# Graph kernel: the keys of the edges are asked for five batches ahead, into six buffers, instead of two batches ahead into three

## The chip, the cores and the metric

The program runs on one core of a Trainium2 chip. The metric is device time in microseconds (us), from one launch of the whole program. Engines are called as the profile calls them: PE (TensorE), DVE (VectorE), ACT (ScalarE), POOL (GpSimd), SP (SyncE).

## The reference

The input is a graph of 1250 nodes with 768 features and 20000 edges, sorted by target node. A GCN layer (layer 0) is followed by a relational graph attention module of two layers, with 4 heads (layer 1) and 1 head (layer 2), and three relations. Both parts are residual.

```python
def rgat_conv(x, W, q, k, b, src, dst, etype, heads, out_ch, n_nodes):
    xr = jnp.einsum('nd,rdf->rnf', x, W)
    oi = xr[etype, dst]
    oj = xr[etype, src]
    qi = oi @ q
    kj = oj @ k
    alpha = jax.nn.leaky_relu(qi + kj, NEG_SLOPE)
    m = jax.ops.segment_max(alpha, dst, num_segments=n_nodes)
    e = jnp.exp(alpha - m[dst])
    z = jax.ops.segment_sum(e, dst, num_segments=n_nodes)
    a = e / (z[dst] + EPS)
    msg = (a[:, :, None] * oj.reshape(-1, heads, out_ch)).reshape(-1, heads * out_ch)
    out = jax.ops.segment_sum(msg, dst, num_segments=n_nodes)
    return out + b
...
h = jnp.maximum(_layernorm(x, axis=-1), 0.0)
x = x + _L0_gnn_ref(h, edge_index, L0_gnn_W, L0_gnn_b)
h = jnp.maximum(_layernorm(x, axis=-1), 0.0)
x = x + _L1_gnn_ref(h, edge_index, edge_type_3, ...)
```

## The kernel before, in words

The 1250 nodes are 10 tiles of 128. The sorted edges lie in slots, 128 to a column. Two columns are a pair, and a pair holds edges of one target tile only. These inputs fill 83 pairs. The target tiles are very uneven: the first has 26 pairs (0 to 25), the second 11 (26 to 36), the third 8 (37 to 44), and the last seven have 7, 6, 6, 5, 5, 5 and 4.

Each attention layer l (1 and 2) has these parts. All of them but the last run in one stretch, which the rest of this text calls the score stretch of the layer.

- POOL fetches, for each column of 128 edges, the key `kj` of each edge's source from a table in DRAM, by one indirect DMA per column (`ask_keys`, line L519). Twelve columns (6 pairs) are a batch. When a batch is there, `score` adds the query and applies the leaky ReLU in three short POOL instructions (L529, L533, L537), which release the batch's six pairs to DVE through the semaphore `al_step`. The number of gathers in flight is bounded by separate semaphores, `k_in`, of which there are `KFLIGHT`: 4 in layer 1, 2 in layer 2. Gather t waits until gather t - 4 (or t - 2) has landed. Thirteen batches (0 to 12, `KSURE`) are written out one after the other, the last one (13) is in a loop whose count depends on the data, and ran once here. The batches lie in `kb`, which has `KSEMS` slots.
- DVE gets the queries of the edges ready (`qs_ready`, behind L977) and then builds, pair by pair, the running maximum of each target tile: a subtraction or addition (L1017 in layer 1, L1023 in layer 2), and a maximum (L1020, L1028). After the last pair of a tile it raises `z_in`, and `maxima` finishes the tile before (L990 to L996).
- PE multiplies the nodes by the three relations' weights, 30 steps of one node tile each (`project`, L1320). After some of the steps it also turns a tile's running maximum around (L1338) and spreads finished maxima back to the edges (L1236, L1233). These places are fixed, in the order of PE's program, by the table `MAX_AT`: tile 0 after step 11, tile 1 after step 14, tile 2 after step 17, then after steps 19, 21, 23, 25, 27, 28, and the last after step 29. PE waits there for `z_in`, and for the reading of the tile before.
- The last part gathers whole rows of 768 features (L488, POOL), scales them (DVE) and sums them with one-hot matmuls (PE, L1359 or L1361 and L1362). POOL can't begin before PE has passed all of the maxima and DVE has formed the exponents' arguments (the semaphore of L1348).

POOL's order in the score stretch is: wait for the keys' table, ask for two batches, wait for `qs_ready`, then score batch n and ask for batch n + 2, until 13 batches are asked for and scored. The places in the code are these.

```python
MAX_AT = {11: (0,), 14: (1,), 17: (2,), 19: (3,), 21: (4,), 23: (5,), 25: (6,), 27: (7,), 28: (8,), 29: (9, 10, 11)}
...
KSEMS = 3
KFLIGHT = {1: 4, 2: 2}
```

Of the kernel before, what the change touches and what calls it, by code (L numbers as in the profile page):

```python
# [40 lines left out]
NPAIR = R * NT * PAIRS_STEP  # L41
KB = 4 * PAIRS_STEP
KBATCHES = 2 * NPAIR // KB
KSEMS = 3
KFLIGHT = {1: 4, 2: 2}
assert all(KB % n == 0 for n in KFLIGHT.values())
assert KBATCHES * KB == 2 * NPAIR
KSURE = ((E + PAIR - 1) // PAIR - 1) // (KB // 2)
# [54 lines left out]
def gnn_kernel(nc, x, src, dst, edge_type, W0, b0, W1, q1, k1, b1, W2, q2, k2, b2, out):  # L103
# [12 lines left out]
    with ExitStack() as ctx:  # L116
# [124 lines left out]
        qe = ringf[:, 0:T * R * 4]  # L241
        kb = ringf[:, T * R * 4:T * R * 4 + KSEMS * KB * 16].rearrange("p (a t c) -> p a t c", a=KSEMS, c=16)

# [99 lines left out]
        def load_bounds(eng):  # L343

            eng.wait_ge(bounds_ready, 1)
            return [0] + [eng.value_load(bounds[0:1, j:j + 1], min_val=j if j < NT else (E + PAIR - 1) // PAIR, max_val=MAXPAIRS) for j in range(1, NT + 1)]
# [107 lines left out]
        @block.gpsimd  # L454
        def _(pool):
            nc.gpsimd.iota(iota_f[:, :], [[1, T]], base=0, channel_multiplier=0, allow_small_or_imprecise_dtypes=True).then_inc(pool_c, 1)
            nc.gpsimd.iota(iota_h[:, :], [[1, T]], base=0, channel_multiplier=0, allow_small_or_imprecise_dtypes=True).then_inc(pool_c, 1)
            nc.gpsimd.iota(iota_p[:, :], [[0, 1]], base=0, channel_multiplier=1, allow_small_or_imprecise_dtypes=True).then_inc(pool_c, 1)
            nc.gpsimd.memset(half[:, :], -0.5).then_inc(pool_c, 1)
            nc.gpsimd.memset(zero16[:, :], 0.0).then_inc(pool_c, 1)  # L460
            nc.gpsimd.memset(ones[:, :], 1.0).then_inc(pool_c, 1)
            nc.gpsimd.memset(idxr[:, T:T + KB], 0).then_inc(pool_c, 1)
            pool.wait_ge(pool_c, 7)
            bnd = load_bounds(pool)
            pool.wait_ge(slots_f, 1)
            pool.sem_inc(turn, 1)

            def targets(first, end):
                for c in range(first * PB, end * PB):

                    pool.wait_ge(perm_free, c + PB + 1)
                    pool.sem_inc(turn, 1)
                    nc.gpsimd.tensor_scalar(oh_tg[:, c % PB, :], iota_h[0:EP, 0:P], dloc[:, c:c + 1], None, ALU.is_equal).then_inc(tg_in, 1)  # L473

            targets(0, 1)
            pool.wait_ge(var_ready, 1)
            nc.gpsimd.tensor_tensor(rstd[:, :], vare[:, :], half[:, :], ALU.pow).then_inc(rstd_ready, 1)
            targets(1, GROUPS)
            pool.wait_ge(deg_ready, 1)
            nc.gpsimd.tensor_tensor(dinv[:, :], deg[:, :], half[:, :], ALU.pow).then_inc(dinv_ready, 1)  # L480
            groups = (bnd[NT] + (RING - 1)) // RING
            rest = (bnd[NT] + (RING - 1 - RING * FIXED)) // RING

            def gather_rows(l, idx):

                for t in range(2 * RING * FIXED):
                    pool.wait_ge(w_used[l], t + 1)
                    nc.gpsimd.indirect_dma_start(ring[:, t % (2 * RING), 0:WIDTH[l]], None, rows[l], bass.IndirectOffsetOnAxis(idx[:, t:t + 1], 0)).then_inc(g_sem[l][t % (2 * RING)], 16)  # L488

                with pool.Fori(0, rest) as g:  # L490
                    for side in range(2):

                        pool.wait_ge(g_in[l], 2 * RING * g + (2 * RING * FIXED + RING * side + 1))
                        nc.gpsimd.tensor_copy(idxs[:, RING * side:RING * (side + 1)], idx[:, ds(g * (2 * RING) + (2 * RING * FIXED + RING * side), RING)]).then_inc(ix[l], 1)
                        pool.wait_ge(ix[l], 2 * g + (side + 1))
                        pool.sem_inc(turn, 1)
                        for s in range(RING * side, RING * (side + 1)):
                            if s % 2 == 0:

                                pool.wait_ge(w_used[l], g * (2 * RING) + (2 * RING * FIXED + s + 2))  # L500
                                pool.sem_inc(turn, 1)
                            nc.gpsimd.indirect_dma_start(ring[:, s, 0:WIDTH[l]], None, rows[l], bass.IndirectOffsetOnAxis(idxs[:, s:s + 1], 0)).then_inc(g_sem[l][s], 16)

            pool.wait_ge(slots_ready, 1)
            pool.wait_ge(s_rows0, 16 * (NT + 1))
            gather_rows(0, idx0)
            pool.wait_ge(var_ready, 2)
            nc.gpsimd.tensor_tensor(rstd[:, :], vare[:, :], half[:, :], ALU.pow).then_inc(rstd_ready, 1)
            for l in (1, 2):
                H = HEADS[l]  # L510

                flight = KFLIGHT[l]

                def ask_keys(n):

                    for t in range(n * KB, (n + 1) * KB):
                        if t >= flight:
                            pool.wait_ge(k_in[l][t % flight], 16 * (t // flight))
                        nc.gpsimd.indirect_dma_start(kb[:, n % KSEMS, t % KB, 0:4], None, keys[l], bass.IndirectOffsetOnAxis(idxr[:, t:t + 1], 0)).then_inc(k_in[l][t % flight], 16)  # L519

                def score(n, slot, lows, looped=False):

                    batch = al[:, ds(n * (KB * H), KB * H)]
                    for s in range(flight):
                        pool.wait_ge(k_in[l][s], n * (16 * KB // flight) + 16 * KB // flight)
                    if looped or n > 0:
                        pool.wait_ge(al_step[l], n * (KB // 2))
                    pool.sem_inc(turn, 1)
                    nc.gpsimd.tensor_tensor(summed[:, 0:KB * H].rearrange("p (c h) -> p c h", h=H), kb[:, slot, :, 0:H], qs[:, ds(n * (KB * H), KB * H)].rearrange("p (c h) -> p c h", h=H), ALU.add).then_inc(k_sum[l], 1)  # L529
                    pool.wait_ge(k_sum[l], n + 1)  # L530
                    if looped:
                        pool.sem_inc(turn, 1)
                    nc.gpsimd.tensor_scalar(low[:, 0:KB * H], summed[:, 0:KB * H], 0.0, SLOPE - 1.0, ALU.min, ALU.mult).then_inc(k_low[l], 1)  # L533
                    pool.wait_ge(k_low[l], lows)
                    if looped:
                        pool.sem_inc(turn, 1)
                    nc.gpsimd.tensor_tensor(batch, summed[:, 0:KB * H], low[:, 0:KB * H], ALU.add).then_inc(al_step[l], KB // 2)  # L537

                pool.wait_ge(g_in[l - 1], 2 * RING * groups + (RING + 1))
                pool.sem_inc(turn, 1)  # L540
                pool.wait_ge(s_keys, 16 * R * l)
                ask_keys(0)
                ask_keys(1)
                pool.wait_ge(qs_ready, l)
                for n in range(KSURE):
                    score(n, n % KSEMS, n + 1)
                    if n + 2 < KSURE:
                        ask_keys(n + 2)


                with pool.Fori(1, (bnd[NT] + (255 - (KSURE + 1) * (KB // 2))) // 256 + 2) as m:
                    n = m + (KSURE - 1)
                    nc.gpsimd.tensor_copy(idxk[:, :], idxr[:, ds(n * KB, KB)]).then_inc(k_low[l], 1)
                    pool.wait_ge(k_low[l], m * 2 + (KSURE - 1))
                    pool.sem_inc(turn, 1)
                    for k in range(KB):
                        pool.wait_ge(k_in[l][k % flight], n * (16 * KB // flight) + 16 * (k // flight))
                        pool.sem_inc(turn, 1)
                        nc.gpsimd.indirect_dma_start(kb[:, KSURE % KSEMS, k, 0:4], None, keys[l], bass.IndirectOffsetOnAxis(idxk[:, k:k + 1], 0)).then_inc(k_in[l][k % flight], 16)
                    score(n, KSURE % KSEMS, m * 2 + KSURE, True)  # L560
                for side in range(2):
                    pool.wait_ge(stage_out[l][side], 16 * R * NT // 2)
                pool.wait_ge(rows_go[l], 1)
                gather_rows(l, idxr)
# [826 lines left out]
```

## Time and profile before

| | us |
|---|---|
| median of the runs | 1615.69 |
| the runs | 1609.24, 6044.12, 1615.69 |
| the profiled execution | 1607.11 |
| its span, first to last instruction | 1605.3 |
| mean granted TensorE clock in it | 0.932 of full |

The rows below come from the profiled execution. Its span is 1.8 us shorter than its time; the median of the runs is 8.6 us above it. One of the three runs lies far off the others and has no part in what follows. Of the span, the score stretch of layer 1 is from 469 us (the first gather of keys) to 780 us (the first gather of rows), that of layer 2 from 1063 us to 1365 us.

A row of a timeline gives the start in us, the duration in us, the engine, the line, the operation, what it writes and reads, how many equal instructions the row stands for, and in brackets how long the engine had been idle and what ended that.

### The profile page before, as it was taken

The page shows a single profiled execution, that of the slowest core. Times are in us where ns is not written, and L with a number is a line of the kernel's source. Part 1 is how long each engine was busy: PE and PEld are TensorE (multiplying, and loading weights), DVE is VectorE, ACT ScalarE, POOL GpSimd, SP SyncE. Part 2 cuts the span into 40 slices and gives each one's busy share as a digit, 9 for nine tenths or more (in the row PEclk, how much of TensorE's full clock was granted, in tenths as well). Part 3 has the DMA queues.
Part 4 walks back from the last instruction along what each step waited for, and adds up shares of the span by engine and source line. Part 5 has one row for each costly group of instructions (what it writes and reads, how often), then busy time and mean ns, then how long its engine had stood idle before and what let it go on. Part 6 is the DMA issues. An engine that isn't in the chain of part 4 may idle for free.

```text
span 1605.3 us, 24837 instructions
## 1 busy us (share of the span) xinstructions
PE 1453.7 (91%) x6446; PEld 878.0 (55%) x6450; DVE 901.0 (56%) x2002; ACT 274.0 (17%) x709; POOL 1000.9 (62%) x1112
## 2 busy tenths in 40 slices
PE   4988999999978999999699999769996999899996
PEld 2545555555566555666455555455553655455553
DVE  8677722334455888888688878406324445223333
ACT  2545300000011333323000124410110011000000
POOL 1599277666537777882477777336656662777673
PEclk9988999999987999899799999858997999899998
DMA  8300498899831131111588888701231111889898
GB/s 319 118 20 21 125 315 305 291 316 312 270 102 23 51 110 47 40 37 41 169 303 278 285 262 257 241 3 32 59 111 31 40 43 50 286 298 308 281 303 269
DMA packets 86811, 271.80 MB, mean 169 GB/s; under 512 B 32156, under 2 KB 32531, under 8 KB 86743
## 3 DMA queue, kind: packets, MB, share of 16 engines
q0 software_dynamic: 51072, 199.44, 39.3%
q1 hardware_dynamic: 34807, 65.62, 11.4%
q10 hardware_dynamic: 864, 5.90, 1.0%
q8 instruction: 35, 0.57, 0.2%
q14 instruction: 33, 0.27, 0.1%
HBM read 239.28 MB, written 31.62 MB: 169 GB/s over the span
## 4 chain that ended last, share of the span: by engine, by line
PE 61%; DMA 14%; POOL 10%; issue 7%; DVE 5%; ACT 1%; DVEq 1%; SPq 0%; POOLq 0%; ACTq 0%; PEldq 0%
PE ps L1293 12%; PE ps L1320 12%; PE ps L1359 12%; DMA ring<-keys,idxr 8%; POOL ring L519 8%; PE ps L1361 6%; PE ps L1362 6%; PE ps L1190 5%; DMA ring<-rows,idxr 3%; PE ps L1111 1%; PE ps L1236 1%; PE ps L1153 1%; PE ps L1254 1%; DVE zw L1020 1%; DVE hn L1017 1%
## 5 line engine op out<-in xcount | busy, mean ns | idle before, releaser
L1320 PE MATMUL ps<-wreg,hT 128*128 128x384 f32 x1440 | 486.7, 501 | 7.3 <-PEq L1313 6.6
L519 POOL DMA_INDIRECT ring<-keys,idxr x312 | 319.2, 1023 | 189.1 <-DMA ring<-keys,idxr 73.6
L488 POOL DMA_INDIRECT ring<-rows,idxr x304 | 303.7, 999 | 168.8 <-PEq L1348 60.9
L1320 PEld LDWEIGHTS ps<-wreg,hT 128*128 128x128 f32 x1440 | 280.6, 196 | 202.2 <-issue 23.5
L1359 PE MATMUL ps<-ring,zw 128*128 x664 | 224.0, 495 | 15.6 <-DVE zw L1088 15.0
L1293 PE MATMUL ps<-ring,zw 128*128 x664 | 221.3, 495 | 9.6 <-DVE zw L909 9.6
L488 POOL DMA_INDIRECT ring<-rows,idx x152 | 144.7, 952 | 97.1 <-PE ps L1293 66.0
L1359 PEld LDWEIGHTS ps<-ring,zw 128*128 128x128 f32 x664 | 124.7, 191 | 108.7 <-issue 34.2
L1086 DVE TENSOR_TENSOR ring<-ring,al x166 | 159.2, 959 | 39.4 <-SPq L406 30.7
L1293 PEld LDWEIGHTS ps<-ring,zw 128*128 128x128 f32 x664 | 127.5, 193 | 98.1 <-issue 15.3
L1091 DVE TENSOR_SCALAR zw<-iota_f,tl,al 128x128 f32<-128x128 f32 x166 | 60.8, 368 | 154.7 <-PE ps L1362 129.7
L909 DVE TENSOR_SCALAR zw<-iota_f,tl,ring 128x128 f32<-128x128 f32 x166 | 58.6, 358 | 154.8 <-PE ps L1293 140.0
L1361 PE MATMUL ps<-ring,zw 128*128 x332 | 136.3, 492 | 9.9 <-DVE zw L1091 9.7
L473 POOL TENSOR_SCALAR stT<-iota_h,stT 125x128 f16<-125x128 f16 x160 | 106.4, 683 | 49.7 <-DVEq L799 28.1
L1362 PE MATMUL ps<-ring,zw 128*128 x332 | 135.2, 489 | 0.0
L1017 DVE TENSOR_TENSOR hn<-al,hn 128x1024 f32 x83 | 101.7, 1225 | 35.4 <-POOL al L537 15.5
L1023 DVE TENSOR_TENSOR hn<-hn,al 128x256 f32 x83 | 35.6, 429 | 143.8 <-POOL al L537 127.8
L1020 DVE TENSOR_TENSOR zw<-zw,hn 128x1024 f32<-128x1024 f32 x83 | 101.8, 1227 | 2.9
L1361 PEld LDWEIGHTS ps<-ring,zw 128*128 128x128 f32 x332 | 62.5, 191 | 53.4 <-issue 13.5
L1362 PEld LDWEIGHTS ps<-ring,zw 128*128 128x128 f32 x332 | 63.4, 191 | 44.3 <-issue 0.6
L1190 PE MATMUL ps<-ring,hT 128*128 128x384 f32 x240 | 86.0, 513 | 0.0
L659 ACT ACTIVATE hn<-iota_f,tlb 128x128 f32<-128x128 f32 (+1 forms) x166 | 56.8, 393 | 119.2 <-DVE hn L1017 105.7
(189 smaller groups left out, 1314.0 us busy)
## 6 DMA issues: line engine op xcount, KB each, us to landing
wreg<-in_L_gnn_W SPq DMA_DIRECT2D x11, 2304.0 KB, 9.8
rows<-stage SPq DMA_DIRECT2D x30, 386.0 KB, 2.8
rows<-stage SPq DMA_DIRECT2D x30, 384.5 KB, 2.9
stT<-targets_row ACTq DMA_DIRECT2D x6, 960.0 KB
ring<-keys,idxr POOLq DMA_INDIRECT x312, 2.5
ring<-rows,idxr POOLq DMA_INDIRECT x304, 4.5
rows<-stT SPq DMA_DIRECT2D x10, 384.0 KB, 2.9
xs<-in_x SPq DMA_DIRECT2D x3, 1152.0 KB, 13.4
```

The source lines that it names most:

```text
L473: nc.gpsimd.tensor_scalar(oh_tg[:, c % PB, :], iota_h[0:EP, 0:P], dloc[:, c:c + 1], None, ALU.is_equal).then_inc(tg_in, 1)
L488: nc.gpsimd.indirect_dma_start(ring[:, t % (2 * RING), 0:WIDTH[l]], None, rows[l], bass.IndirectOffsetOnAxis(idx[:, t:t + 1], 0)).then_inc ...
L519: nc.gpsimd.indirect_dma_start(kb[:, n % KSEMS, t % KB, 0:4], None, keys[l], bass.IndirectOffsetOnAxis(idxr[:, t:t + 1], 0)).then_inc(k_in ...
L1017: V.tensor_tensor(scored[:, :, 0:H, :], scores_at(i, 0, H, 2).rearrange("p (b h) -> p b h", b=2).unsqueeze(3).to_broadcast([P, 2, H, P]), ...
L1020: V.tensor_tensor(run, run, scored[:, :, 0:H, :], ALU.max).then_inc(m_chain[l], 1)
L1086: V.tensor_tensor(row, row, scores_at(i, b, H).unsqueeze(2).to_broadcast([P, H, ROW // H]), ALU.mult).then_inc(rows_scaled, 1)
L1190: last = mm(ps[:, 4 - 2 * (nt % 2) + h, 0:HALF], hT[:, k, nt * P:(nt + 1) * P], w0s[:, k, h * HALF:(h + 1) * HALF], start=(k == 0), stop=( ...
L1293: last = mm(ps[:, 2 * (j % 2) + a, 0:HALF], zw[:, 0, b, 0, :], row_at(i, b, a * HALF, (a + 1) * HALF), start=False, stop=False, skip_group ...
L1320: last = mm(ps[:, 2 * (nt % 2) + h, 0:HALF], hT[:, k, nt * P:(nt + 1) * P], wreg[:, r % 2, k, h * HALF:(h + 1) * HALF], start=(k == 0), st ...
L1359: last = mm(ps[:, 2 * (j % 2) + a, 0:2 * W], zw[:, 0, b, 0, :], row_at(i, b, a * 2 * W, (a + 1) * 2 * W), start=False, stop=False, skip_gr ...
L1361: mm(ps[:, 2 * (j % 2), 0:HALF], zw[:, 0, b, 0, :], row_at(i, b, 0, HALF), start=False, stop=False, skip_group_check=True)
L1362: last = mm(ps[:, 2 * (j % 2) + 1, 0:HALF + 1], zw[:, 0, b, 0, :], row_at(i, b, HALF, D + 1), start=False, stop=False, skip_group_check=True)
```

## The change

`KSEMS` goes from 3 to 6, so `kb` has six slots, and a new constant `AHEAD = 5` takes the place of the lead of two: five batches are asked for ahead of the wait for `qs_ready` and of the first `score`, and batch n + 5 is asked for behind `score(n)`. `KFLIGHT` stays. The number of gathers, of scores and of all other instructions stays too. A line is added near the top, so every later line has a number greater by one in the changed kernel.

```diff
-KSEMS = 3
+KSEMS = 6
+AHEAD = 5
 KFLIGHT = {1: 4, 2: 2}
...
                 pool.wait_ge(g_in[l - 1], 2 * RING * groups + (RING + 1))
                 pool.sem_inc(turn, 1)
                 pool.wait_ge(s_keys, 16 * R * l)
-                ask_keys(0)
-                ask_keys(1)
+                for n in range(AHEAD):
+                    ask_keys(n)
                 pool.wait_ge(qs_ready, l)
                 for n in range(KSURE):
                     score(n, n % KSEMS, n + 1)
-                    if n + 2 < KSURE:
-                        ask_keys(n + 2)
+                    if n + AHEAD < KSURE:
+                        ask_keys(n + AHEAD)
```

Only POOL's order changes. At the start of the score stretch of layer 1 POOL's program has, before the change, these rows (`DMA ring<-keys` are the gathers of keys, since `kb` lies in the memory of `ring`; `summed`, `low` and `al` are the three instructions of a score):

```order
L508 TENSOR_TENSOR rstd<-vare,half 128x10
L539 ISA
L519 DMA ring<-keys,idxr 128x4 x24
L529 TENSOR_TENSOR summed<-ring,etmp 128x48
L533 TENSOR_SCALAR low<-summed 128x48
L537 TENSOR_TENSOR al<-summed,low 128x48
L519 DMA ring<-keys,idxr 128x4 x12
```

and after it these, at the same place:

```order
L509 TENSOR_TENSOR rstd<-vare,half 128x10
L540 ISA
L520 DMA ring<-keys,idxr 128x4 x60
L530 TENSOR_TENSOR summed<-ring,etmp 128x48
L534 TENSOR_SCALAR low<-summed 128x48
L538 TENSOR_TENSOR al<-summed,low 128x48
L520 DMA ring<-keys,idxr 128x4 x12
```

The 36 gathers of batches 2, 3 and 4 have moved ahead of the score of batch 0. At the end of POOL's written-out batches the program of before has the scores of batches 10, 11 and 12 with the last written-out gathers between the first two of them:

```order
L519 DMA ring<-keys,idxr 128x4 x12
L529 TENSOR_TENSOR summed<-ring,etmp 128x48
L533 TENSOR_SCALAR low<-summed 128x48
L537 TENSOR_TENSOR al<-summed,low 128x48
L519 DMA ring<-keys,idxr 128x4 x12
L529 TENSOR_TENSOR summed<-ring,etmp 128x48
L533 TENSOR_SCALAR low<-summed 128x48
L537 TENSOR_TENSOR al<-summed,low 128x48
L529 TENSOR_TENSOR summed<-ring,etmp 128x48
L533 TENSOR_SCALAR low<-summed 128x48
L537 TENSOR_TENSOR al<-summed,low 128x48
```

and the changed one has the scores of batches 8 to 12 there in a row, of which these are the first four:

```order
L520 DMA ring<-keys,idxr 128x4 x12
L530 TENSOR_TENSOR summed<-ring,etmp 128x48
L534 TENSOR_SCALAR low<-summed 128x48
L538 TENSOR_TENSOR al<-summed,low 128x48
L530 TENSOR_TENSOR summed<-ring,etmp 128x48
L534 TENSOR_SCALAR low<-summed 128x48
L538 TENSOR_TENSOR al<-summed,low 128x48
L530 TENSOR_TENSOR summed<-ring,etmp 128x48
L534 TENSOR_SCALAR low<-summed 128x48
L538 TENSOR_TENSOR al<-summed,low 128x48
L530 TENSOR_TENSOR summed<-ring,etmp 128x48
L534 TENSOR_SCALAR low<-summed 128x48
```

No gather stands between these scores any more. Layer 2 has the same rows with 128x12 instead of 128x48.

## Rows read from the trace of the kernel before

**Rows 1.** The page: span, and the chain that ended last, by engine

```profile
span 1605.3 us, 24837 instructions
PE 61%; DMA 14%; POOL 10%; issue 7%; DVE 5%; ACT 1%; DVEq 1%; SPq 0%; POOLq 0%; ACTq 0%; PEldq 0%
```

**Rows 2.** POOL's waits over the span: us in total, times, longest us

```profile
POOL ring L519 <- DMA ring<-keys,idxr: 73.6, 108, 5.0
...
POOL ring L488 <- PEq L1348: 60.9, 2, 41.2
...
POOL summed L529 <- DMA ring<-keys,idxr: 0.6, 1, 0.6
```

**Rows 3.** Timeline of POOL, score stretch of layer 1

```profile
498.60 0.94 POOL L519 DMA_INDIRECT ring<-keys,idxr  x1 [0.30 <-issue]
499.85 0.94 POOL L519 DMA_INDIRECT ring<-keys,idxr  x1 [0.30 <-issue]
...
501.74 0.28 POOL L537 TENSOR_TENSOR al<-summed,low 128x48 f32<-128x48 f32 x1
...
556.11 0.28 POOL L537 TENSOR_TENSOR al<-summed,low 128x48 f32<-128x48 f32 x1
...
573.60 0.28 POOL L537 TENSOR_TENSOR al<-summed,low 128x48 f32<-128x48 f32 x1
...
612.12 0.28 POOL L537 TENSOR_TENSOR al<-summed,low 128x48 f32<-128x48 f32 x1
```

**Rows 4.** Timeline of DVE, layer 1: queries ready, last pair of tile 0, tile 1 done

```profile
497.18 2.59 DVE L977 TENSOR_REDUCE etmp<-ring 128x720 f32<-128x2160 f32 x1 [0.16 <-DVE ring L970]
...
574.29 1.23 DVE L1017 TENSOR_TENSOR hn<-al,hn 128x1024 f32 x1 [1.44 <-POOL al L537]
...
578.25 1.23 DVE L1020 TENSOR_TENSOR zw<-zw,hn 128x1024 f32<-128x1024 f32 x1
...
615.54 1.22 DVE L990 TENSOR_REDUCE mx<-ps 128x4 f32<-128x1024 f32 x1
```

**Rows 5.** Timeline of PE, score stretch of layer 1

```profile
592.50 1.04 PE L1338 MATMUL ps<-ident,zw 128*128 128x128 f32 x8
...
616.91 1.07 PE L1338 MATMUL ps<-ident,zw 128*128 128x128 f32 x8
617.81 23.39 PE L1320 MATMUL ps<-wreg,hT 128*128 128x384 f32 x72
...
778.01 0.18 PE L1241 MATMUL ps<-zero 128*128 128x8 bf16 x1
```

**Rows 6.** DVE's waits for POOL: first 617 to 776 us, then the score stretch of layer 2

```profile
DVE hn L1017 <- POOL al L537: 2.4, 5, 0.5
...
DVE hn L1023 <- POOL al L537: 127.8, 13, 15.5
```

**Rows 7.** Timeline of POOL, score stretch of layer 2

```profile
1062.74 0.94 POOL L519 DMA_INDIRECT ring<-keys,idxr  x1 [38.01 <-DMA keys<-kst]
...
1097.10 0.98 POOL L529 TENSOR_TENSOR summed<-ring,etmp 128x12 f32<-128x12 f32 x1
...
1099.18 0.23 POOL L537 TENSOR_TENSOR al<-summed,low 128x12 f32<-128x12 f32 x1 [0.15 <-POOL low L533]
...
1157.52 0.21 POOL L537 TENSOR_TENSOR al<-summed,low 128x12 f32<-128x12 f32 x1
...
1219.48 0.21 POOL L537 TENSOR_TENSOR al<-summed,low 128x12 f32<-128x12 f32 x1
...
1345.17 0.21 POOL L537 TENSOR_TENSOR al<-summed,low 128x12 f32 x1 [0.25 <-POOL low L533]
```

**Rows 8.** Timeline of PE, score stretch of layer 2

```profile
1185.11 0.38 PE L1338 MATMUL ps<-ident,zw 128*128 128x128 f32 x2
1185.32 23.39 PE L1320 MATMUL ps<-wreg,hT 128*128 128x384 f32 x72
1222.02 0.66 PE L1338 MATMUL ps<-ident,zw 128*128 128x128 f32 x2 [13.31 <-DVE mx L990]
1222.47 26.10 PE L1320 MATMUL ps<-wreg,hT 128*128 128x384 f32 x72
...
1363.02 0.17 PE L1241 MATMUL ps<-zero 128*128 128x8 bf16 x1
```

**Rows 9.** PE's projection line in two windows: window, length, PE and PEld busy (count), granted clock

```profile
1185.00:1209.00 24.00, 23.65 (x73) 13.60 (x72) 1.00 0.28 88
1222.00:1248.00 26.00, 25.53 (x71) 15.03 (x72) 0.89 0.13 32
```

## The prediction

> **What bounds the kernel now.** I read the page's chain first [rows 1]: PE has most of it, POOL with its transfers a quarter. A share doesn't say which wait ends last in a stretch, so I then took the two score stretches one by one, since only they hold the moved instructions. The waits of POOL come next [rows 2]. POOL waits 73.6 us in all for landings of gathers of keys, and the reader is to see where: ahead of a next gather (L519), for the landing of the one four or two places before it. Ahead of a score (L529) it waits once, 0.6 us. So with two batches of lead the keys of a batch are always there when its score comes. The wait of 60.9 us for L1348, which is all of POOL's waiting at the ends of the two score stretches, says that POOL is done early there and the rows' gathers hang on PE and DVE.
>
> Then the timelines of the three engines, laid side by side. In layer 1 the queries are ready at 499.8 [rows 4] and the 24 gathers asked for ahead of them are out at 500.8 [rows 3]: the lead of two ends one us after what it waits beside. DVE gets tile 0's last two pairs (24 and 25, in batch 4, whose score ends at 573.9) and finishes them at 579.5 [rows 3, 4]. PE arrives for that tile at 592.5, 13.0 us later, without waiting. Tile 1's last pair is 36, the first of batch 6; that score ends at 612.4, the tile is done at 615.5, and PE turns it at 616.9, with 1.4 us to spare [rows 3 to 5]. From there PE and DVE go neck and neck to 778: the first has 15 steps of projection and the spreads, and DVE waits only 2.4 us for POOL in the whole rest [rows 6]. That is, from 617 on neither has air in it. In layer 2 DVE has little work and waits 127.8 us for POOL [rows 6], while PE stands 13.3 us ahead of tile 1 [rows 8], because batch 6 is scored at 1219.7 [rows 7]. After that PE isn't held up to 1363.0. POOL's last score of the layer ends at 1345.4 and holds nobody.
>
> So in both layers the time is set by one point: when batch 6 is scored. PE has 15 of its 30 steps behind that point and works through them at its own pace.
>
> **The change part by part.**
>
> The buffers. Three more slots cost no instruction. They would pay if POOL waited for a free slot or a score waited for landings; there is no such wait but the 0.6 us [rows 2]. The number in flight is bounded by KFLIGHT, which stays, so each gather waits for the landing four or two before it, as now. Gain: 0 to 0.6 us, I take 0.
>
> The order, layer 1. Batches 2, 3 and 4 move ahead of the first score: 36 gathers. One takes 0.94 us and 0.30 us between, 1.25 us from start to start, while DVE is idle [rows 3]; DVE is idle then, as it waits for the first score. 36 x 1.25 = 45.0 us, so score 0 ends at 502.0 + 45.0 = 547.0 instead of 502.0. The price can't be below 45 by that row. Above, the nearest row is the pace beside a working DVE: from score 0 at 502.0 to score 3 at 556.4 are three batches and three scores in 54.4 us [rows 3]; without the scores, of 1.2 us each (from the end of the last gather at 500.8 to 502.0), that is 51 us. I take 45, since DVE is idle.
>
> Behind score 0 the pace is as before, since 12 gathers still stand between two scores up to score 8 (batch 12 is asked for behind score 7). So scores 4 and 6 come 45 us later too: 618.9 and 657.4. Only scores 9 to 12 come in a burst behind score 8, with no gathers between, and no sooner than now: POOL's total is the same. What is late next: tile 0 done at 579.5 + 45 = 624.5. PE is there at 592.5 and stands 32 us. Tile 1 done at 615.5 + 45 = 660.5, PE turns it at about 662, not 617. PE's work behind it is untouched and DVE's has no slack to give back (2.4 us). Sum for layer 1: +45 us, and by the bounds +43 (DVE's 2.4 recovered) to +51. The cover that was there, PE's 13.0 us ahead of tile 0, is no help, because tile 1 had 1.4.
>
> The order, layer 2. With two in flight the pace is slower and hangs on landings. From score 0 (1099.4) to score 3 (1157.7) there are exactly the 36 gathers and three scores: 58.3 us [rows 7]. At 1.2 us a score, as in layer 1, the gathers are 54.6 us. The other end: 24 gathers from 1062.74 to 1097.10 [rows 7], 1.43 us each, part of them beside a quiet machine; 36 of these are 51.5 us. I take 53. Score 6 then ends at 1219.7 + 53 = 1272.7 and PE turns tile 1 at 1275 instead of 1222.0. PE has no wait behind it now and gets none: tile 2 (last pair 44, batch 7) is there about 19 us after score 6, before PE's three steps of 26 us are over; scores 8 to 12 come together. POOL's last score stays near 1345, and PE's end goes from 1363.0 to 1416. Sum: +53 us, bounds +51.5 and +55.
>
> The clock of PE. PE now stands 32 us ahead of tile 0 and about 13 us ahead of tile 1 in layer 1, where it didn't stand. What a stand costs beyond itself is in the trace: three steps took 23.39 us before the 13.3 us wait and 26.10 us behind it, at a granted clock of 1.00 and 0.89 [rows 8, 9], so part of them ran at 1.2 GHz instead of 2.4 GHz. That is 2.7 us. Behind tile 0's wait it is hidden by the wait for tile 1; behind tile 1's wait it counts in layer 1, as new. In layer 2 tile 1's wait is there already. Sum +2.7, bounds 0 and 5.4 (if the longer waits of 32 and 50 us leave as much over again). The page "TensorE: Matmul & The Clock Gate" of the Trainium skill, Part 1, says that an idle TensorE falls back to half clock and returns to full once it has been busy; by that rule each new wait has a price of this kind, and the trace agrees in direction with its 0.89.
>
> The keys' transfers themselves. "DMA: Bandwidth & Descriptors" of the Trainium skill, in its section on the anatomy of one DMA, gives each of POOL's DMAs a fixed cost near 2 us, most of it the confirmation of the landing. By it a longer lead is the remedy, if a consumer sits out that latency. The trace has the latency's wait ahead of scores at 0.6 us; the sum stays as it is, and the rival that follows has its chance from that.
>
> Total: 45 + 53 + 2.7 = 100.7 us. The profiled execution is at 1607.1, which gives 1707.8. The median of the runs is 8.6 us above it, the fastest run 2.1 us. I put the forecast at 1710.
>
> **The rivals.**
>
> A deeper lead hides landings (faster). If the waits of 73.6 us went, batch 6 in layer 2 would be scored earlier and PE's 13.3 us would go, with its 2.7 us of clock, and 2.4 us in layer 1: 1607 - 18 = 1589, 1.1% below. For it speaks that POOL's pace up to score 6 is what PE's wait in layer 2 hangs on. Against it: those waits stand ahead of gathers, on semaphores that the change leaves alone, and moving batches forward makes the first score wait for more of them. It decides only if the limit were slots. To be over 2% faster it would have to give 32 us, more than any wait that it could remove. Chance 2%, of which faster by over 2% is 1%.
>
> The delay is absorbed (within 2%). POOL's last score ends when it did, and if DVE and PE could catch up, the stretches would end as now: 1607. It would be so if the ends hung on POOL's last batch, as layer 2's gap of 18 us between 1345.4 and 1363.0 might suggest. Against it: PE can't do a projection of step 12 before it has turned tile 0, by the order of its program, and it has 15 steps, some 140 us, behind tile 1 in both layers. Only if the pause of PE were filled with those steps would the time be kept. Chance 4%.
>
> The change doesn't do what its words say. It says six semaphores, and KFLIGHT, which counts the semaphores that gathers wait on, is not touched; the effect is a pure reorder. I count that as part of the forecast.
>
> The damage is larger (slower still). If the three steps behind each wait ran at half clock as a whole, they would take up to 46.8 us instead of 23.4. At worst that is 23 us in each layer, on top, less the hidden part: 1710 + 35 = 1745. Against it is the one wait in the trace, with 2.7 us. Or the gathers ahead run slower, since the writes of projected rows share the queues: 5 to 6 us. Chance 6%.
>
> **How the numbers follow.** Forecast 88%, larger damage 6%, absorbed 4%, lead pays 2%. The terms' bounds give 43 + 51.5 + 0 = 94.5 and 51 + 55 + 5.4 = 111.4 over 1607.1, so 1702 to 1719; the offset between an execution's profile and a median may add 9, and an error in how PE and DVE share the end of layer 1 some us to either side: 1692 to 1727. That range holds over 8 in 10, the small cases left out. About 2% (32 us) is what a measurement of this kernel can tell from no change. Slower by over 2%: 94%. Within: 5%. Faster: 1%.
>
> **What would show it.** In the changed profile, the first score (L530) starts near 546 in layer 1 and some 53 us later than 1097 in layer 2. PE waits for DVE at tile 0, about 32 us in layer 1 and about 50 us in layer 2, and again at tile 1, 13 to 18 us; before, these came to 0, 0, 0 and 13.3. The time from PE's turning of tile 1 to its last spread is 161 us in layer 1 and 141 us in layer 2, give or take 5. POOL's waits for landings ahead of gathers stay near 74 us in total. DVE's waits for POOL ahead of its first pair grow. Nothing changes outside of the two stretches. The prediction is wrong if PE's wait at tile 0 is missing, if the gathers ahead of score 0 go much faster than 1.25 us each, or if PE's work behind tile 1 shrinks.

## The result, and the profile after

The changed kernel takes 1702.72 us (median of 4 runs, 1698.41 to 1705.66), the kernel before 1616.05 us beside it. The 6044.12 us run is in that second median and not in the ratio, which is 1.0549, with a 95% interval of 1.0505 to 1.0593: slower by 5.5%, some 88 us. The profiled execution of the changed kernel has a span of 1703.8 us, 98.5 us more than the one of before [rows 1]. That is more than 88 us because of which executions were profiled: the slowest of the four of the changed kernel (1705.66 us), and one of the kernel before that took less (1607.11 us) than its runs here. In the later comparisons the kernel before had medians of 1605 to 1612 us; against these the changed kernel is 91 to 97 us slower.

The page of the changed kernel (span, and the chain that ended last, by engine) and POOL's waits over the span:

```profile
span 1703.8 us, 24837 instructions
PE 59%; DMA 14%; POOL 12%; issue 8%; DVE 5%; ACT 1%; DVEq 0%; SPq 0%; POOLq 0%; ACTq 0%; PEldq 0%
```

```profile
POOL ring L489 <- PEq L1349: 168.7, 2, 98.4
POOL ring L520 <- DMA ring<-keys,idxr: 73.2, 113, 3.2
...
POOL summed L530 <- DMA ring<-keys,idxr: 0.3, 1, 0.3
```

Against rows 2, the waits for landings stand where they were: 73.2 us after 73.6, ahead of the next gather, and next to nothing ahead of a score. The new thing is that POOL, done with its scores no later than before, now waits 168.7 us instead of 60.9 for PE and DVE to finish the stretches. The 107.8 us more are the 99.4 us by which the two stretches grew and the 8.4 us by which POOL's last scores came earlier in them.

POOL in the score stretch of layer 1 (ends of scores 0, 4 and 6):

```profile
545.38 0.29 POOL L538 TENSOR_TENSOR al<-summed,low 128x48 f32<-128x48 f32 x1
...
617.24 0.29 POOL L538 TENSOR_TENSOR al<-summed,low 128x48 f32<-128x48 f32 x1
...
655.74 0.29 POOL L538 TENSOR_TENSOR al<-summed,low 128x48 f32<-128x48 f32 x1
```

PE in the same stretch (the second row is cut off at the end of its view), and the waits of PE from 440 to 860 us:

```profile
496.81 21.32 PE L1321 MATMUL ps<-wreg,hT 128*128 128x384 f32 x60 [3.57 <-PEq L1314]
548.56 13.65 PE L1321 MATMUL ps<-wreg,hT 128*128 128x384 f32 x37 [30.42 <-ACT stage L688]
...
627.07 1.04 PE L1339 MATMUL ps<-ident,zw 128*128 128x128 f32 x8
...
660.53 1.94 PE L1339 MATMUL ps<-ident,zw 128*128 128x128 f32 x8 [6.95 <-DVE mx L991]
662.27 24.33 PE L1321 MATMUL ps<-wreg,hT 128*128 128x384 f32 x72
...
826.22 0.18 PE L1242 MATMUL ps<-zero 128*128 128x8 bf16 x1
```

```profile
PE ps L1321 <- ACT stage L688: 34.2, 5, 30.4
PE ps L1339 <- DVE mx L991: 12.1, 3, 6.9
```

The stretch began 2.2 us earlier here (466.85 us instead of 469.04). Counted from there, score 0 ends 45.8 us later than before, score 6 45.8 us later, and tile 1 is turned 45.8 us later [rows 3, 5]. PE lost that time, but not at the place that I had named. It stood 30.4 us after only two and a half steps of projection (60 of the first 288 matmuls that stand ahead of tile 0), for ACT's copy of its results, at tile 0 it didn't stand at all, and at tile 1 only 7.0 us. ACT's own timeline says why (a copy of projected rows, then a mask):

```profile
502.69 0.58 ACT L688 ACTIVATE stage<-ps,rstd 128x384 f32<-128x384 f32 x1 [30.75 <-PE ps L1321]
547.35 0.69 ACT L660 ACTIVATE hn<-iota_f,tlb 128x128 f32<-128x128 f32 x2 [44.07 <-DVE hn L1018]
```

In layer 1 ACT makes the masks for the pairs between its copies, and each mask waits until DVE has used the one two pairs before. DVE had no score before 546 us, so ACT sat in the mask of the third pair with PE's results waiting behind it.

POOL in the score stretch of layer 2 (first gather, ends of scores 0, 6 and the last):

```profile
1110.42 0.94 POOL L520 DMA_INDIRECT ring<-keys,idxr  x1 [37.54 <-DMA keys<-kst]
...
1201.12 0.21 POOL L538 TENSOR_TENSOR al<-summed,low 128x12 f32<-128x12 f32 x1 [0.15 <-POOL low L534]
...
1319.47 0.21 POOL L538 TENSOR_TENSOR al<-summed,low 128x12 f32<-128x12 f32 x1
...
1391.15 0.21 POOL L538 TENSOR_TENSOR al<-summed,low 128x12 f32 x1 [0.25 <-POOL low L534]
```

and PE:

```profile
1283.93 0.69 PE L1339 MATMUL ps<-ident,zw 128*128 128x128 f32 x2 [50.97 <-DVEq L1031]
1284.41 25.57 PE L1321 MATMUL ps<-wreg,hT 128*128 128x384 f32 x72
1322.01 0.66 PE L1339 MATMUL ps<-ident,zw 128*128 128x128 f32 x2 [12.03 <-DVE mx L991]
1322.46 25.32 PE L1321 MATMUL ps<-wreg,hT 128*128 128x384 f32 x72
...
1459.67 0.18 PE L1242 MATMUL ps<-zero 128*128 128x8 bf16 x1
```

Counted from the first gather of the stretch, score 0 ends at 90.9 us instead of 36.7, score 6 at 209.3 instead of 157.0, and POOL's last score at 280.9 instead of 282.6 [rows 7]. PE stands 51.0 us at tile 0 and 12.0 us at tile 1 [rows 8]. The time behind tile 1, to the last spread, is 137.7 us after 141.0: nothing was won back there but 3.3 us.

### The profile page after: what moved, and what is told of

It is laid out like the page before. It is cut to its first block, busy times and chain, and to the rows that moved or that the text cites. A ratio compares the mean times of both kernels' runs of the same rounds, so it can differ in the third digit from the quotient of the medians.

```text
span 1703.8 us, 24837 instructions
## 1 busy us (share of the span) xinstructions
PE 1461.3 (86%) x6446; PEld 880.3 (52%) x6450; DVE 900.1 (53%) x2002; ACT 273.4 (16%) x709; POOL 991.5 (58%) x1112
## 4 chain that ended last, share of the span: by engine, by line
PE 59%; DMA 14%; POOL 12%; issue 8%; DVE 5%; ACT 1%; DVEq 0%; SPq 0%; POOLq 0%; ACTq 0%; PEldq 0%
PE ps L1321 13%; PE ps L1360 13%; PE ps L1294 11%; POOL ring L520 10%; DMA ring<-keys,idxr 9%; PE ps L1362 5%; PE ps L1191 5%; PE ps L1363 5%; DMA ring<-rows,idxr 1%; PE ps L1112 1%; DMA ring<-rows,idxs 1%; PE ps L1237 1%; PE ps L1154 1%; PE ps L1255 1%; DMA keys<-kst 1%
## 5 line engine op out<-in xcount | busy, mean ns | idle before, releaser
L1321 PE MATMUL ps<-wreg,hT 128*128 128x384 f32 x1440 | 492.6, 504 | 41.7 <-ACT stage L688 34.2
L489 POOL DMA_INDIRECT ring<-rows,idxr x304 | 300.8, 989 | 281.3 <-PEq L1349 168.7
L520 POOL DMA_INDIRECT ring<-keys,idxr x312 | 315.7, 1012 | 186.9 <-DMA ring<-keys,idxr 73.2
L1360 PEld LDWEIGHTS ps<-ring,zw 128*128 128x128 f32 x664 | 125.8, 193 | 108.3 <-issue 33.4
L1087 DVE TENSOR_TENSOR ring<-ring,al x166 | 159.1, 958 | 37.5 <-SPq L407 25.9
L1362 PE MATMUL ps<-ring,zw 128*128 x332 | 136.9, 494 | 11.5 <-DVE zw L1092 11.5
L1018 DVE TENSOR_TENSOR hn<-al,hn 128x1024 f32 x83 | 101.7, 1225 | 83.5 <-POOL al L538 58.6
L1024 DVE TENSOR_TENSOR hn<-hn,al 128x256 f32 x83 | 35.5, 427 | 159.9 <-POOL al L538 143.5
L1021 DVE TENSOR_TENSOR zw<-zw,hn 128x1024 f32<-128x1024 f32 x83 | 101.8, 1226 | 2.9
```

The source lines that it names most:

```text
L1018: V.tensor_tensor(scored[:, :, 0:H, :], scores_at(i, 0, H, 2).rearrange("p (b h) -> p b h", b=2).unsqueeze(3).to_broadcast([P, 2, H, P]), ...
L1021: V.tensor_tensor(run, run, scored[:, :, 0:H, :], ALU.max).then_inc(m_chain[l], 1)
L1087: V.tensor_tensor(row, row, scores_at(i, b, H).unsqueeze(2).to_broadcast([P, H, ROW // H]), ALU.mult).then_inc(rows_scaled, 1)
L1321: last = mm(ps[:, 2 * (nt % 2) + h, 0:HALF], hT[:, k, nt * P:(nt + 1) * P], wreg[:, r % 2, k, h * HALF:(h + 1) * HALF], start=(k == 0), st ...
L1360: last = mm(ps[:, 2 * (j % 2) + a, 0:2 * W], zw[:, 0, b, 0, :], row_at(i, b, a * 2 * W, (a + 1) * 2 * W), start=False, stop=False, skip_gr ...
L1362: mm(ps[:, 2 * (j % 2), 0:HALF], zw[:, 0, b, 0, :], row_at(i, b, 0, HALF), start=False, stop=False, skip_group_check=True)
```

## The experiments

Each was timed beside the kernel before, in interleaved runs on the same chip. The ratios are not quotients of the two medians; the two differ by up to 0.2%. The table has, for each kernel, the ratio to the kernel before with its 95% interval, and from its trace: the length of the two score stretches (first gather of keys to first gather of rows) and the ends of scores 0 and 6, counted from the stretch's start, in us.

| kernel | median, before beside it | ratio | layer 1: stretch, score 0, score 6 | layer 2: stretch, score 0, score 6 |
|---|---|---|---|---|
| before | | | 311.1, 33.0, 143.4 | 302.3, 36.7, 157.0 |
| changed | 1702.72, 1616.05 | 1.0549 [1.0505, 1.0593] | 361.5, 78.8, 189.2 | 351.3, 90.9, 209.3 |
| buffers | 1607.97, 1605.28 | 1.0020 [1.0003, 1.0038] | 313.5, 34.2, 145.7 | 297.4, 35.6, 155.2 |
| l1_only | 1652.81, 1605.28 | 1.0291 [1.0264, 1.0319] | 355.8, 78.6, 187.0 | 301.2, 36.1, 157.3 |
| l2_only | 1654.48, 1605.28 | 1.0295 [1.0264, 1.0327] | 316.0, 34.5, 145.2 | 345.4, 87.3, 203.8 |
| burst | 1642.81, 1605.28 | 1.0219 [1.0189, 1.0249] | 351.5, 79.2, 150.6 | 303.0, 87.1, 157.7 |
| ahead3 | 1635.62, 1609.06 | 1.0170 [1.0132, 1.0207] | 325.2, 48.0, 156.5 | 315.5, 51.9, 172.5 |
| ahead1 | 1653.31, 1609.06 | 1.0255 [1.0213, 1.0298] | 331.9, 33.6, 155.7 | 331.6, 30.5, 159.7 |
| masks_later | 1696.22, 1609.06 | 1.0539 [1.0496, 1.0582] | 399.1, 78.0, 188.9 | 302.8, 36.0, 156.7 |
| masks_later2 | 1660.86, 1611.71 | 1.0284 [1.0233, 1.0335] | 359.8, 79.2, 190.8 | 302.0, 37.1, 156.9 |
| flight4 | 1591.03, 1609.06 | 0.9889 [0.9854, 0.9923] | 311.6, 33.4, 143.8 | 282.0, 32.8, 134.4 |
| flight6 | 1590.22, 1611.71 | 0.9877 [0.9851, 0.9902] | 315.4, 34.1, 143.5 | 283.3, 32.8, 133.1 |
| flight4_ahead5 | 1671.38, 1611.71 | 1.0379 [1.0353, 1.0404] | 354.6, 77.9, 186.4 | 321.6, 78.4, 180.3 |

Each kernel has one trace. The stretch of a layer with the same code in it scatters by 5 to 7 us between traces (layer 1 unchanged 311.1 to 316.0, with a lead of five 354.6 to 361.5; layer 2 unchanged 297.4 to 303.0, with a lead of five 345.4 and 351.3), so differences below that say nothing.

**The buffers alone.** The kernel before with

```diff
-KSEMS = 3
+KSEMS = 6
```

> Six slots for the keys, but the lead stays two batches: the order of every engine is that of the kernel before. My theory (the moved gathers cost all of it, the slots give nothing): the time of the kernel before, within 3 us. Rival (the slots alone free POOL of waits): up to 18 us faster, since POOL's waits for landings ahead of gathers, 73.6 us in all before, would shrink.

2.7 us more, 0.2%. The slots give nothing, and cost next to nothing. POOL's waits for landings ahead of gathers are still 69.8 us; the rival is out.

**One layer at a time.** The changed kernel with a lead for each layer, `AHEAD = {1: 5, 2: 2}` and `{1: 2, 2: 5}`:

```diff
-                for n in range(AHEAD):
+                for n in range(AHEAD[l]):
                     ask_keys(n)
...
-                    if n + AHEAD < KSURE:
-                        ask_keys(n + AHEAD)
+                    if n + AHEAD[l] < KSURE:
+                        ask_keys(n + AHEAD[l])
```

> The lead is five batches in layer 1 and two in layer 2, six slots. My theory: 36 gathers of 1.25 us ahead of layer 1's first score, 45 us, and 3 to 5 us for TensorE's clock behind the new waits: 47 to 51 us over the kernel before. Layer 2's stretch (first gather of keys to last spread) stays at 300 us. Rival (layer 1 has slack, since layer 2 gets back what layer 1 loses or the other way round): less than 40 us.

> The lead is two batches in layer 1 and five in layer 2, six slots. My theory: 36 gathers ahead of layer 2's first score, 49 to 54 us over the kernel before; the two single-layer kernels together make up the whole loss of the changed kernel, 97 us or so. Rival: the two parts don't add up, by over 8 us.

47.5 us and 49.2 us over the kernel before, each just inside what was expected. The layer that isn't touched keeps its stretch within the scatter. Together they make 96.7 us, and added as ratios 1.0586, which is inside the interval of the changed kernel (1.0505 to 1.0593), near its upper end. Between the medians of its own comparison the changed kernel lost only 86.7 us, so by that the parts miss by 10 us; against the kernel before of the later comparisons it lost 91 to 97. That the two losses are nearly equal is shown; that they add up is shown to within 10 us, and no part of one is seen in the other layer.

**Late first score, punctual fourth.** The decisive one for the mechanism:

```diff
-                    if n + AHEAD < KSURE:
-                        ask_keys(n + AHEAD)
+                    if n >= 3 and n + 2 < KSURE:
+                        ask_keys(n + 2)
```

> Five batches are asked for ahead of the first score, as in the changed kernel, but then scores 0 to 3 follow without gathers between, and from there on batch n + 2 is asked for behind score n, as in the kernel before. So the first score is late by the same 36 gathers, and score 4 and all behind it are as early as before. Theory A (what counts is when batch 6 is scored, and in layer 1 the chain of VectorE, which has 2.7 us of work for each pair and can't catch up): layer 1 loses about 33 us (VectorE's work of 256 us from 547 us on), layer 2, where VectorE needs 1.4 us for a pair and waits for most of the time, loses 0 to 3 us. Total 33 to 38 us over the kernel before. Theory B (a late first score costs its lateness in both layers): 95 us over, as the changed kernel.

37.5 us over. In layer 2, POOL (ends of score 0, of score 3 and of score 6) and PE at tile 1:

```profile
1192.66 0.21 POOL L538 TENSOR_TENSOR al<-summed,low 128x12 f32<-128x12 f32 x1 [0.15 <-POOL low L534]
...
1197.14 0.21 POOL L538 TENSOR_TENSOR al<-summed,low 128x12 f32<-128x12 f32 x1
...
1263.35 0.21 POOL L538 TENSOR_TENSOR al<-summed,low 128x12 f32<-128x12 f32 x1
```

```profile
1265.89 0.66 PE L1339 MATMUL ps<-ident,zw 128*128 128x128 f32 x2 [13.16 <-DVE mx L991]
```

The first score of layer 2 is 50.4 us late, and the layer loses nothing: 303.0 us after 302.3. Score 6 is at 157.7 us, where it was, and PE's wait at tile 1 is the 13 us of before. Theory B is out, and in layer 2 theory A is shown: it is batch 6 that counts. In layer 1 score 6 is only 7 us late, and yet the stretch is 40.4 us longer: there DVE's chain, 2.7 us for each pair, starts 46 us late and has too little idle time to catch up. Up to tile 1 DVE had waited 13.1 us for POOL in the kernel before; in burst, once score 0 is there, it waits 0.6 us. I had expected 33; PE turned tile 1 36.1 us later, and 4.3 us came behind it, in a trace of the slowest of burst's four runs (1652.15 us, where the median is 1642.81).

**Other leads.** The changed kernel with `AHEAD = 3` and with `AHEAD = 1`.

> A lead of three in both layers, six slots: 12 gathers more ahead of the first score than before. Theory (each batch of lead over two costs its own gathers' time): 15 us in layer 1 and 17 in layer 2, up to 3 for the clock: 30 to 36 us over the kernel before, a third of the changed kernel's loss. Rival (there is a threshold, a cover that hides a small lead): less than 15 us.

> A lead of one in both layers: 12 gathers fewer ahead of the first score. POOL then waits for the queries, and ahead of each score for the landing of the batch's last gather, some 2 us each time, as nothing lies between. Theory: the first score comes at most 1 us earlier in layer 1 and 8 in layer 2, score 6 later by 12 us and 5 us: 10 to 35 us over the kernel before. Rival (less lead is better throughout): faster than the kernel before by 10 us or more.

A lead of three costs 26.6 us, under the 30 to 36 expected; in the traces layer 1 loses 14.1 us and layer 2 13.2 us, where I had 15 and 17. Score 6 is late by 13.1 and 15.5 us, about the time of 12 gathers, so there is no cover for a small lead. A lead of one costs 44.3 us, more than the 10 to 35 expected. Its cost is of another kind, as POOL's waits show:

```profile
POOL summed L530 <- DMA ring<-keys,idxr: 47.4, 24, 6.3
```

Now POOL waits for the landing ahead of nearly every score, 2 us a time. Score 6 is late by 12.3 and 2.7 us only, but POOL's last score of layer 2 ends at 311.5 us instead of 282.6, and the stretch is 29.3 us longer. PE, which had no wait behind tile 1 in this layer, now has one just behind that score (it ends at 1394.7):

```profile
1396.95 0.66 PE L1339 MATMUL ps<-ident,zw 128*128 128x128 f32 x2 [11.47 <-DVE mx L991]
```

I had left out that POOL's end, harmless before, comes onto the path when POOL itself gets slower. So two is the best of the four leads tried.

**ACT's masks.** Is PE's wait for ACT a loss of its own? The kernel with a lead of five in layer 1 alone, and

```diff
-MASKS_AT = [(SURE_PAIRS - 3) * (h + 1) // LAST_PAIRS_AT + 2 for h in range(LAST_PAIRS_AT)]
+MASKS_AT = [2 + 2 * max(0, h - 11) if h < 24 else 26 + -(-11 * (h - 23) // 6) if h < 30 else 37 + 41 * (h - 29) // 25 for h in range(LAST_PAIRS_AT)]
```

> As the kernel with a lead of five in layer 1 alone, but ScalarE makes the masks of layer 1's pairs later: none but the first two pairs' up to its 12th copy of projected rows, and then on a steeper table, so that ScalarE isn't caught in a wait for VectorE's first pair while TensorE's results wait for their copy. In the changed kernel TensorE stood 30.4 us for ScalarE's copy at 518 to 549 us. Theory A (that wait only takes the place of the one for tile 0; the late score 6 sets the time either way): the 30.4 us wait is gone, waits appear later, up to tile 0, and the time is within 4 us of the lead of five in layer 1 alone. Theory B (ScalarE's waiting adds to the loss): at least 10 us less than with that kernel.

Both theories missed. The wait for ACT went, PE stood 30.5 us at tile 0 in its place, and tile 1 was turned 197.2 us into the stretch, 5.6 us behind the kernel with five in layer 1 alone. So far that is theory A. But behind that the kernel lost another 40 us (87.2 us over the kernel before, where five in layer 1 alone lost 47.5). DVE's waits from 495 to 870 us say where:

```profile
DVE hn L1018 <- ACT hn L660: 53.8, 10, 14.1
DVE hn L1018 <- POOL al L538: 52.6, 5, 44.9
```

My table gave the masks of each tile only just in time for PE to need them. While PE stood at a tile, ACT had no more copies to place masks behind, and DVE ran out of masks. The experiment had a fault of its own, so it was repeated with a table that catches up:

```diff
-MASKS_AT = [(SURE_PAIRS - 3) * (h + 1) // LAST_PAIRS_AT + 2 for h in range(LAST_PAIRS_AT)]
+MASKS_AT = [2 if h < 12 else 2 + 13 * (h - 11) // 6 if h < 24 else 28 + 5 * (h - 23) // 2 if h < 30 else (SURE_PAIRS - 3) * (h + 1) // LAST_PAIRS_AT + 2 for h in range(LAST_PAIRS_AT)]
```

> Again a lead of five in layer 1 alone with ScalarE's masks started at its 12th copy, but now the table catches up by the time of tile 1 (43 pairs by the 29th copy, as the table of the kernel before), so that VectorE isn't starved of masks behind tile 0. Theory A (the wait for ScalarE in the changed kernel stands in for the one at tile 0, and score 6 sets the time): TensorE stands some 30 us at tile 0 and 10 to 15 us at tile 1, and the time is within 6 us of the lead of five in layer 1 alone, 1647 to 1659 us. Theory B (the late masks cost by themselves wherever they are, as in the first table, which took 44 us more): over 10 us more.

The ratio is 1.0284 against 1.0291 with the table of the kernel before. PE at tiles 0 and 1:

```profile
628.93 1.97 PE L1339 MATMUL ps<-ident,zw 128*128 128x128 f32 x8 [30.18 <-DVEq L1031]
...
666.69 1.94 PE L1339 MATMUL ps<-ident,zw 128*128 128x128 f32 x8 [10.88 <-DVE mx L991]
```

The 30 us stand at tile 0 now, as in the prediction, and the ratio is the same (the median, 1660.86 us, is 2 us above the 1647 to 1659 expected, beside a kernel before that was 6 us slower than the one of l1_only). The wait for ACT is one more place at which the same lateness of DVE is paid, not a cost beside it.

**The number in flight.** What could have paid, instead of the lead. The kernel before with

```diff
-KFLIGHT = {1: 4, 2: 2}
+KFLIGHT = {1: 4, 2: 4}
```

> The kernel before, with a lead of two and three slots, but with four gathers of keys in flight in layer 2 instead of two. Theory A (the number in flight, not the lead, sets POOL's pace in layer 2, where it waits for landings ahead of gathers): a batch takes 16 to 17 us instead of 19.5, batch 6 is scored before TensorE comes to tile 1, TensorE's wait of 13.3 us goes: 11 to 17 us under the kernel before. Theory B (the landings are slowed by the other transfers, whatever is in flight): no change, within 3 us.

18.0 us less, ratio 0.9889 [0.9854, 0.9923]: a gain of 1.1%, clear of the noise and a little over the 11 to 17 us expected. POOL's waits for landings fall from 73.6 us [rows 2] to

```profile
POOL ring L519 <- DMA ring<-keys,idxr: 11.5, 26, 2.1
```

(nearly all of the 73.6 us lay in layer 2, 67.5 us). Each such idle time, though, has in it the 0.3 us that POOL pauses between any two gathers, so by estimate some 40 of the 73.6 us were real waiting (73.6 - 108 x 0.3). PE reaches tile 1 of layer 2 without a wait, at full pace on both sides of it:

```profile
1179.18 23.39 PE L1320 MATMUL ps<-wreg,hT 128*128 128x384 f32 x72
1202.40 0.38 PE L1338 MATMUL ps<-ident,zw 128*128 128x128 f32 x2
1202.62 23.39 PE L1320 MATMUL ps<-wreg,hT 128*128 128x384 f32 x72
```

Score 6 comes 22.6 us earlier, the stretch is 20.4 us shorter. This is faster than both kernels of the change. Then six in flight in both layers, `KFLIGHT = {1: 6, 2: 6}`, and the changed kernel with four in layer 2:

> The kernel before, lead of two and three slots, with six gathers of keys in flight in both layers. Theory (four already leave POOL bound by its own issue of 1.25 us, and score 6 ahead of TensorE in layer 2): the time of the kernel with four in flight in layer 2, within 4 us, so 14 to 22 us under the kernel before. Rival (the 11.5 us that POOL still waits for landings are on the path): another 5 to 11 us less.

> The changed kernel (lead of five in both layers) with four gathers in flight in layer 2 instead of two. Theory: layer 1 as in the changed kernel, 45 to 50 us over the kernel before; in layer 2 the 36 gathers ahead of score 0 cost 1.3 us each, 46 us, of which the 9 us that four in flight had put score 6 ahead of TensorE are hidden: some 37 to 42 us over the kernel with four in flight and a lead of two. In all 82 to 92 us over that kernel, 65 to 75 over the kernel before. Rival (with four in flight the lead pays or is free): less than 60 us over the kernel with four in flight.

Six gives what four gives (0.9877 against 0.9889): POOL is bound by its own issue by then, as none of its idle times for a landing ahead of a gather of keys is over 0.3 us. The lead of five costs with four in flight too. Layer 2's stretch grows from 282.0 to 321.6 us, 39.6 us, within the 37 to 42 expected: score 6 moves by 45.9 us, and part of that is hidden, as PE used to come to tile 1 later than DVE's signal there. Against the kernel before the loss is 59.7 us, under the 65 to 75 expected. Against flight4 it is 80 us between the medians and 78 us when each is set against its own kernel before, under the 82 to 92 expected; the two stretches in the traces differ by 82.7 us. The rival's 60 us are clearly passed.

## Why the prediction was right

- **What bounds the kernel.** Right. That the time hangs on when batch 6 is scored is shown for layer 2 by burst (score 0 late, score 6 punctual, no loss) and by flight4 (score 6 early, 20 us won). For layer 1 it was too narrow: there DVE's chain from its first pair on counts, and burst lost 40.4 us with score 6 only 7 us late. In the changed kernel both are late by the same 45.8 us, so the sum was not touched by it. The 1.4 us to spare at tile 1 were misread as well: PE waits there for the end of DVE's L990, 616.8 us, not for its start, so it had 0.15 us [rows 4, 5].
- **Buffers: 0 taken.** 0.2%, by the kernel with the slots alone.
- **Layer 1: 45 us taken.** Score 0, score 6 and tile 1's turning all moved by 45.8 us, 1.27 us for each of the 36 gathers. The row of 1.25 us a gather carried over, as DVE was idle. The stretch grew by 50.4 us.
- **Layer 2: 53 us taken, bounds 51.5 to 55.** Score 0 moved by 54.2 us (60 gathers in 90.0 us, 1.50 us each), score 6 and tile 1's turning by 52.3. The stretch grew by 49.0 us only, under the lower bound: PE's time behind tile 1 was 3.3 us shorter than before. That is within the scatter of a stretch, and its cause was not looked for.
- **Where PE stands.** Half wrong. I named tile 0 in layer 1, 32 us. By the prediction's own last paragraph the missing wait at tile 0 was a sign of being wrong. PE stood 30.4 us for ACT, more than nine steps earlier; I hadn't followed ACT's masks, which wait for DVE. In layer 2, where ACT makes no masks, it was 51.0 us at tile 0, as forecast (about 50), and 12.0 at tile 1. The 13 to 18 us forecast for tile 1 came in neither layer: layer 1 had 7.0. masks_later2 puts the wait at tile 0 in layer 1 too, at the same time.
- **The clock: 2.7 us taken.** Behind tile 1 layer 1 took 165.7 us instead of 161.1, 4.6 more, and layer 2 137.7 instead of 141.0. Together 1.3 us, against a scatter of 5 to 7. The three steps behind tile 1, which the term was made of, took 24.33 us in layer 1 at a granted clock of 0.96, against 23.39 without a wait, so 0.9 us is what the new wait cost there; in layer 2 they took 25.32 us after 26.10. The term was too large, and its effect on the whole can't be told from nothing here.
- **The rivals.** That a lead hides landings is out: the waits for landings stayed at 73.2 us. That the delay is absorbed since POOL's last score is punctual is out as well. It was punctual (280.9 after 282.6 us), and POOL only waited for longer behind it. The larger damage didn't come: in the changed kernel no three steps behind a wait took more than 25.57 us, far from 46.8, and the gathers moved ahead of score 0 went at 1.27 us each in layer 1 and 1.5 in layer 2, as forecast. That the writes of projected rows share the queues of the gathers, as that rival had it, is shown by no run.
- **The sum.** 100.7 us over the profiled execution, measured 98.5 between the spans, 88 between the runs that were timed. Some of the closeness is luck: with its clock term layer 1 was put at 47.7 us and grew by 50.4, layer 2 was put at 53 and grew by 49.0, and the two misses nearly cancel. The forecast of 1710 is 7 us above the median, of which 2 us were added to the sum for the offset between a profile and a median, and 5 us are the sum itself. Against the runs beside it the loss of 88 us is 12% less than the sum, against those of the later comparisons 4 to 10% less.

## What to carry to other kernels

A lead in an engine's program order is not free when the same engine both asks and consumes: each batch asked for ahead of the first result delays that result, and what hangs on it, by the time of the batch's whole issue (here 12 gathers of 1.25 to 1.5 us). Raise the lead only until the consumer no longer waits for landings (here two batches: with one, each score waits some 2 us; three already cost 13 to 14 us in each layer). If the issuer waits for landings, look at which semaphore it waits on. Here it was the number in flight, and raising that gave 1.1%, which neither slots nor lead could.

To find out what a delay costs, look behind it for the point at which program order holds the slowest engine with the least to spare (here tile 1 and not tile 0, where PE came 13 us late), and not at the end of the delayed engine's work. Then ask whether an engine between the two, here DVE, has the idle time to catch up.

## What was not expected of the hardware

Two gathers in flight aren't enough for a POOL that can issue one every 1.25 us, though the median from issue to landing is only 2.4 to 2.5 us, just twice that. In layer 2 of the changed kernel the landings take 2.1 to 6.7 us. That it is the late ones that stall the issue is my reading, and no run took it apart. With four in flight the waits fell to 11.5 us in all, and six gave no more. "DMA: Bandwidth & Descriptors" of the Trainium skill (anatomy of one DMA) puts the fixed part of such a DMA near 2 us, mostly the confirmation. The medians here are near that, 0.4 to 0.5 us above; what they are made of no run here shows.

POOL's short operations slow down beside DVE's work in layer 1: L534 takes 0.37 us in some scores and 1.45 us in others, L538 0.28 and 1.02 us, with equal shapes. In the changed kernel L534 is fast in score 6, while DVE stands still from 654.0 to 656.5 us, and slow in score 8, beside DVE's L1018:

```profile
655.22 0.37 POOL L534 TENSOR_SCALAR low<-summed 128x48 f32<-128x48 f32 x1
656.54 1.22 DVE L1018 TENSOR_TENSOR hn<-al,hn 128x1024 f32 x1 [2.53 <-POOL al L538]
...
693.37 1.22 DVE L1018 TENSOR_TENSOR hn<-al,hn 128x1024 f32 x1 [0.22 <-DVE zw L1021]
693.38 1.45 POOL L534 TENSOR_SCALAR low<-summed 128x48 f32<-128x48 f32 x1
```

"SBUF — State Buffer" of the Trainium skill (who interferes with whom) says that a DVE instruction with two inputs in SBUF contends with a POOL instruction that reads SBUF. DVE's L1018 and L1021 are of that kind, and the trace is in accord with that; no run here took it apart.
